# Seven of twenty B products on GpSimd replaced by scalings in token layout, two more C products on GpSimd

## The chip, the cores and the metric

One core of a Trainium2 chip. The metric is the device time of one execution, in microseconds. The kernel before was run three times without the profiler: 3344.13, 3342.19 and 3343.15 us, median 3343.15. The names of the engines in rows: PE is TensorE (PEld its weight loads), DVE is VectorE, ACT is ScalarE, POOL is GpSimd, SP is the engine that issues most DMAs.

## The reference, cut to what matters

```
xn = layernorm(x)                                  # x: 32 batch rows, 512 tokens, 256 channels
for each of two directions (forward, backward in time), with its own weights:
    delta, B, C = split(xn @ x_proj_w.T)           # 32, 16 and 16 columns
    delta = softplus(delta @ dt_proj_w.T + dt_proj_b)      # token x 256
    for each of 16 states n:
        h_t = exp(delta_t * A_n) * h_(t-1) + delta_t * B_t,n * xn_t
        y_t += h_t * C_t,n
    y += D * xn
g = silu(xn + 0.3 * (one expert's MLP of xn, the expert chosen by the last token))
out = x + (y_forward + y_backward) * g
```

## The kernel before

The 32 batch rows are worked one after the other. A row has 32 steps, one for each pair of direction and state (step s is state s mod 16 of direction s div 16). Channels lie on the partitions, in two halves of 128, and the 512 tokens along the free dimension, so that the tensors of a step are 128 x 1024. Each step needs:

- the decay exp(delta * A_n), two activations on ACT (L745, `make_decay`);
- the data delta * xn * B. In 20 of the steps (POOL_B) it is one product on POOL, dx times a broadcast row of B that SP loads from DRAM to all partitions (`times_b`, L473). In the 12 steps of TURNED it comes another way: dx was turned once per direction to token layout (tokens on partitions, `dxT`), ACT scales it by B as a scalar per partition in four activations of 128 x 256 (`scale_dx`, L584), and PE turns the result back with eight transposes into PSUM (`turn_bx`, L1054). In these steps the decay goes to SBUF (`decay_sb`, two slots) and the data to PSUM; in the others the other way round;
- the scan on DVE over time, `hs` (L849), four slots by step;
- the product with C, `hc`. In 13 steps (POOL_C) POOL makes it from a loaded broadcast row of C (L461), four steps after its own step counter (C_LAG), so POOL's step s does the product of step s - 4. In the other 19 DVE makes it (L827), with C broadcast into one PSUM bank by a matmul (`broadcast_c`, L1062), one step after the scan;
- the addition over states in PSUM, eight transposing matmuls on PE (`add_state`, L1079), for POOL's products two steps late (ADD_LAG).

The order of each engine's work is written out by hand: each engine has a `body` that runs over the 32 steps, and waits on semaphores tie them together. Beside the steps each engine does, at fixed step numbers, its part of the front of the next row (layer norm, projections, step size delta, dx, the expert's MLP, the gate): the constants at the top, such as LOG1P = (25, 36) or DX = (28, 43), are the steps, and a number above 31 is a step of the row itself, 32 less. In POOL's part `log1p` is L448, the step size L453, dx L444, the small products of the layer norm L487 to L493, and the residual L480.

Rings tie the engines together around the change. `bx` has RING = 4 slots: `times_b` number i waits for the scan that read number i - 4. `hs` has 4 slots: scan s waits for the product with C of step s - 4, whichever engine makes it. The two PSUM slots `decay0` and `decay1` are used by step parity: what is written for step s waits for scan s - 2. `turn_bx` of step s is issued at PE's step s - 3, ahead of the additions and of PE's front work.

SP issues the loads of B and C rows some products ahead (BRING = 6, CRING = 5), waiting each time for the product that frees the slot, and between them the row's other transfers, all in one queue.

Ahead of the first step lies a prologue of some 84 us: weights, the router, and products of the experts' second layers (`w2`, `wo`), with the front of row 0 in between.

## Time and profile before

| | |
|---|---|
| median of three runs | 3343.15 us |
| the profiled execution | 3348.41 us |
| its span in the trace | 3346.6 us |
| POOL: bx product (L473) | 640, mean 2380 ns |
| POOL: hc product (L461) | 416, mean 2369 ns |
| ACT: scaling of dx (L584) | 1536, mean 497 ns |
| PE: turns (L1054) | 3072 transposes, 435.5 us |
| mean granted clock of TensorE | 0.92 |

The page of the profile gives for each engine the time in which it was busy. The groups by line give count, mean duration and, behind a second bar, the time in which the engine sat idle just before them, with what ended it. Starts in the trace are in microseconds from the beginning of the span; where two instructions of one engine follow each other at once, the distance of their starts is what one takes of the engine, a little less than its duration.

### The profile page before, as it was taken

To read this page: it belongs to the slowest core of one execution; us is meant where nothing else is said; L and a number is where in the kernel's file an instruction comes from. 1 tells how busy PE (TensorE), PEld (TensorE's weight loads), DVE (VectorE), ACT (ScalarE), POOL (GpSimd) and SP (SyncE) were. 2 spreads that over 40 slices of the span, in tenths; PEclk is the share of its full clock that TensorE was granted. 3 is DMA by queue.
4 is the path that set the end of the run, shared out by engine and by line. 5 is a ranking of instruction groups with operands and counts; after the bars stand their busy time and mean duration, and the time that the engine had idled before them with its cause. 6 is when DMAs were issued, how large, how long until landed. Compare 5 with 4: busy or idle time off the path is not lost. (4 is left out here: it accounts for less than half of the span.)

```text
span 3346.6 us, 47865 instructions
## 1 busy us (share of the span) xinstructions
PE 2561.6 (77%) x15542; PEld 2049.9 (61%) x15542; DVE 3116.1 (93%) x2059; ACT 2908.7 (87%) x5370; POOL 3010.0 (90%) x1422
## 2 busy tenths in 40 slices
PE   7777777777777777777777777777777777777776
PEld 5666656666566665566666566666566665666665
DVE  2899999999999999999999999999999999999998
ACT  4888889989888888898888899898898888898985
POOL 2899999999998998999999999999999889999997
PEclk9898999899899988999889999988999889999888
DMA  5443344442344433434433444423434334344332
GB/s 155 137 125 104 100 138 121 128 124 88 119 131 125 125 109 95 132 121 128 125 103 101 136 122 125 126 91 115 130 128 125 106 93 136 119 130 124 96 104 69
DMA packets 273358, 394.09 MB, mean 118 GB/s; under 512 B 45003, under 2 KB 119508, under 8 KB 273108
## 3 DMA queue, kind: packets, MB, share of 16 engines
q1 hardware_dynamic: 273108, 391.03, 38.1%
q8 instruction: 124, 2.03, 0.2%
q14 instruction: 126, 1.03, 0.1%
HBM read 348.98 MB, written 25.18 MB: 112 GB/s over the span
## 5 line engine op out<-in xcount | busy, mean ns | idle before, releaser
L473 POOL TENSOR_TENSOR bx<-dx,b_sb 128x1024 f32<-128x1024 f32 x640 | 1511.8, 2380 | 99.5 <-DVE hs L849 97.7
L849 DVE TENSOR_TENSOR_SCAN hs<-decay,bx 128x1024 f32<-128x1024 f32 x640 | 1458.0, 2280 | 25.5 <-ACT decay L745 8.5
L1079 PE MATMUL y<-ident,hc 128*128 128x128 f32 x8192 | 1145.4, 291 | 25.7 <-DVE hc L827 25.5
L1079 PEld LDWEIGHTS y<-ident,hc 128*128 128x128 f32 x8192 | 1029.9, 152 | 141.2 <-DVE hc L827 80.1
L461 POOL TENSOR_TENSOR hc<-hs,c_sb 128x1024 f32<-128x1024 f32 x416 | 981.0, 2369 | 13.2 <-DVE hs L849 12.9
L849 DVE TENSOR_TENSOR_SCAN hs<-decay_sb,decay 128x1024 f32<-128x1024 f32 x384 | 865.1, 2274 | 77.1 <-issue 38.0
L745 ACT ACTIVATE decay<-delta,rate 128x512 f32<-128x512 f32 (+1 forms) x1280 | 827.3, 683 | 62.1 <-DVE hs L849 61.7
L827 DVE TENSOR_TENSOR hc<-hs,c 128x1024 f32<-128x1024 f32 x608 | 728.7, 1199 | 40.7 <-PE c L1062 36.8
L584 ACT ACTIVATE dxb<-dxT,btok 128x256 f32<-128x256 f32 x1536 | 651.2, 497 | 0.5 <-PE decay L1054 0.5
L1054 PE MATMUL decay<-ident,dxb 128*128 128x128 f32 x3072 | 435.5, 288 | 252.8 <-DVE hs L849 246.4
L1054 PEld LDWEIGHTS decay<-ident,dxb 128*128 128x128 f32 x3072 | 359.7, 147 | 367.5 <-issue 272.7
L1062 PE MATMUL c<-dbc,selector 128*128 128x512 f32 x608 | 327.0, 538 | 324.8 <-DVE hc L827 324.7
L745 ACT ACTIVATE decay_sb<-delta,rate 128x512 f32<-128x512 f32 (+1 forms) x768 | 506.2, 715 | 0.0
L1062 PEld LDWEIGHTS c<-dbc,selector 128*128 128x128 f32 x608 | 125.1, 206 | 407.8 <-DVE hc L827 389.7
L1023 PE MATMUL front<-w2o_sb,hT 128*128 128x256 f32 x1024 | 287.0, 430 | 77.9 <-issue 77.9
L1023 PEld LDWEIGHTS front<-w2o_sb,hT 128*128 128x128 f32 x1024 | 214.7, 221 | 114.2 <-issue 84.4
L1007 PE MATMUL front<-xnT,w_sb 128*128 128x512 f32 x512 | 249.9, 611 | 44.0 <-ACT delta L596 42.8
L448 POOL TENSOR_TENSOR lg<-lg,ex 128x1024 f32<-128x1024 f32 x64 | 151.1, 2362 | 86.9 <-ACT lg L613 86.9
L592 ACT ACTIVATE ex<-front,dtb 128x512 f32<-128x512 f32 x128 | 87.3, 682 | 100.0 <-PE front L998 99.6
L574 ACT ACTIVATE dxT<-front 128x512 f32<-128x512 f32 x128 | 75.8, 592 | 103.3 <-PE front L983 103.1
L619 ACT ACTIVATE hT<-front,b_sb 128x512 f32<-128x512 f32 x128 | 87.7, 685 | 87.3 <-PE front L1007 87.3
L1007 PEld LDWEIGHTS front<-xnT,w_sb 128*128 128x128 f32 x512 | 88.3, 192 | 121.6 <-issue 63.1
(127 smaller groups left out, 2294.4 us busy)
## 6 DMA issues: line engine op xcount, KB each, us to landing
b_sb<-b_scratch SPq DMA_DIRECT2D x640, 256.0 KB, 3.4
c_sb<-b_scratch SPq DMA_DIRECT2D x416, 256.0 KB, 3.6
xin<-in_L_attn_x_dram SPq DMA_DIRECT2D x32, 512.0 KB, 7.7
w_sb<-in_L_ffn_W_dram SPq DMA_DIRECT2D x32, 512.0 KB, 4.3
w2o_sb<-w2o_scratch SPq DMA_DIRECT2D x32, 512.0 KB
xres<-in_L_attn_x_dram SPq DMA_DIRECT2D x32, 512.0 KB, 5.4
out_dram<-og SPq DMA_DIRECT2D x32, 512.0 KB, 4.4
dbc<-high SPq DMA_DIRECT2D x64, 128.0 KB, 5.6
```

The source lines that it names most:

```text
L448: nc.gpsimd.tensor_tensor(lg[:, :, :], lg[:, :, :], ex[:, g, :, :], ALU.mult).then_inc(s_log1p, 1)
L461: nc.gpsimd.tensor_tensor(hc[:, s % RING, :, :], hs[:, s % HSLOTS, :, :], c_sb[:, i % CRING, :].unsqueeze(1).broadcast_to([P, DT, T]), ALU ...
L473: nc.gpsimd.tensor_tensor(bx[:, i % RING, :, :], dx[:, g, :, :], b_sb[:, i % BRING, :].unsqueeze(1).broadcast_to([P, DT, T]), ALU.mult).th ...
L584: A(dxb[:, (row * NT + i) % XSLOTS, c, :], dxT[:, g, c, :], ACT.Copy, scale=btok[:, par, c, g, n:n + 1]).then_inc(s_dxb, 1)
L745: A(to[:, k, cols], delta[:, g * (1 + par), k, cols], ACT.Exp, scale=rate[:, g, k, n:n + 1]).then_inc(s_decay, 1)
L827: V.tensor_tensor(hc[:, s % RING, :, :], hs[:, s % HSLOTS, :, :], cps[:, :].unsqueeze(1).broadcast_to([P, DT, T]), ALU.mult).then_inc(s_hc, 1)
L849: V.tensor_tensor_scan(hs[:, s % HSLOTS, :, :].rearrange("p k t -> p (k t)")[:, u], factor.rearrange("p k t -> p (k t)")[:, u], data.rearr ...
L1007: ins = M(fps[:, :], w1_sb[:, k, j * P:(j + 1) * P], xnT[:, par, k, :], start=(k == 0), stop=(k == DT - 1))
L1023: M(to, hT[:, j, c * P:(c + 1) * P], w2o_sb[:, j, :], start=(j == 0), stop=False)
L1054: ins = nc.tensor.transpose(dps[s % DSLOTS][:, k, c * P:(c + 1) * P], dxb[:, (row * NT + i) % XSLOTS, c, k * P:(k + 1) * P], ident[:, :])
L1062: M(cps[:, :], selector[:, N + n:N + n + 1].broadcast_to([P, P]), dbc[:, par, g, :], start=True, stop=True).then_inc(s_cps, 1)
L1079: ins = M(yps[:, c, k * P:(k + 1) * P], hc[:, s % RING, k, c * P:(c + 1) * P], ident[:, :], start=False, stop=(s == ADDED[-1]), is_transpo ...
```

## The change

GpSimd gets a second way to the data of a step. For seven states (POOL_X = 7, 10, 12, 23, 26, 29, 31), which were full products with B on POOL, POOL scales dx in token layout by B, four `tensor_scalar` of 128 x 256 each into a new buffer `dxp` of two slots, and PE turns them back as it does ACT's. TURNED grows from 12 to 19 states, POOL_B shrinks from 20 to 13. Two more products with C (states 22 and 25) move from DVE to POOL, 15 in place of 13. The ring of bx has 3 slots in place of 4, that of B rows 5 in place of 6. SP's queue runs over steps in place of B products, and moves B and C at step 14. In the prologue the loads of dt_proj come ahead of two larger ones, a memset that they wait for comes first, one activation of the router comes earlier, and the first GELU comes after the first two decays.

```diff
-    BRING, CRING, C_AHEAD = 6, 5, 3
-    TSLOTS, XSLOTS = 2, 3
+    BRING, CRING, C_AHEAD = 5, 5, 3
+    BXRING, TSLOTS, XSLOTS, PSLOTS = 3, 2, 3, 2
...
-    TURNED, SCALED_AT, TURN_LEAD = (5, 6, 8, 9, 11, 13, 14, 15, 22, 24, 28, 30), (0, 2, 3, 4, 5, 7, 9, 10, 17, 19, 23, 25), 3
+    SCALED, SCALED_AT, TURN_LEAD = (5, 6, 8, 9, 11, 13, 14, 15, 22, 24, 28, 30), (0, 2, 3, 4, 5, 7, 9, 10, 17, 19, 23, 25), 3
+    POOL_X, POOL_X_AT = (7, 10, 12, 23, 26, 29, 31), (3, 6, 9, 19, 22, 25, 28)
+    TURNED = sorted(SCALED + POOL_X)
     POOL_B = [s for s in range(STEPS) if s not in TURNED]
-    POOL_C, C_LAG, ADD_LAG = (2, 4, 5, 7, 9, 10, 11, 12, 16, 18, 20, 26, 27), 4, 2
+    POOL_C, C_LAG, ADD_LAG = (2, 4, 5, 7, 9, 10, 11, 12, 16, 18, 20, 22, 25, 26, 27), 4, 2
...
+        dxp = sb("dxp", [P, PSLOTS, C, D])
...
-        bx = sb("bx", [P, RING, DT, T])
+        bx = sb("bx", [P, BXRING, DT, T])
...
             sp.dma_start(xin[:, :, :], x_rows[0]).then_inc(s_x, 16)
             for g, w in enumerate((xw_f, xw_b)):
                 sp.dma_start(xw_raw[64 * g:64 * g + 64, :], w).then_inc(s_xw, 16)
-            sp.dma_start(w2_in[0][:, :, :], w2_v[0]).then_inc(s_w2[0], 16)
-            sp.dma_start(wo_sb[:, :, :], wo.rearrange("(k p) n -> p k n", p=P)).then_inc(s_wo, 16)
             sp.wait_ge(s_dtz, 1)
             for g, w in enumerate((dtw_f, dtw_b)):
                 for a in range(2):
                     sp.dma_start(dtw_raw[:, g, :, 64 * a:64 * a + R], w.rearrange("(k p) r -> p k r", p=P)).then_inc(s_xw, 16)
+            sp.dma_start(w2_in[0][:, :, :], w2_v[0]).then_inc(s_w2[0], 16)
+            sp.dma_start(wo_sb[:, :, :], wo.rearrange("(k p) n -> p k n", p=P)).then_inc(s_wo, 16)
...
-                for i in range(NBX):
-                    j = i + BRING - 1
-                    if j < NBX:
-                        load_b(row, par, j)
...
+                for s in range(STEPS):
+                    if s in POOL_B:
+                        j = on_bx(s) + BRING - 1
+                        if j < NBX:
+                            load_b(row, par, j)
+                        elif not last:
+                            load_b(row + 1, 1 - par, j - NBX)
+                    if s - C_LAG in POOL_C:
+                        i = on_pool(s - C_LAG) + C_AHEAD
+                        if i < NPC:
+                            load_c(row, par, i)
+                        elif not last:
+                            load_c(row + 1, 1 - par, i - NPC)
...
-                used = i - RING
+                used = i - BXRING
                 wait(pool, s_scan, used // NBX * STEPS + POOL_B[used % NBX] + 1)
...
+            def scale_dx(row, par, i):
+                g, n, a = POOL_X[i] // N, POOL_X[i] % N, row * NX + i
+                pool.wait_ge(s_btok, row + 1)
+                pool.wait_ge(s_dxT, row * 4 + g * 2 + 2)
+                if a >= PSLOTS:
+                    pool.wait_ge(s_bxT, turned_before(POOL_X, a - PSLOTS))
+                for c in range(C):
+                    nc.gpsimd.tensor_scalar(dxp[:, a % PSLOTS, c, :], dxT[:, g, c, :], btok[:, par, c, g, n:n + 1], None,
+                                            ALU.mult).then_inc(s_dxp, 1)
...
                     if s in POOL_B:
                         times_b(row, s)
                     if s - C_LAG in POOL_C:
                         times_c(row, s - C_LAG)
+                    if s in POOL_X_AT:
+                        scale_dx(row, par, POOL_X_AT.index(s))
                     front(row, par, s + STEPS)
...
-            gelu(0)
-            act.preload_act_table_set(exp_ln)
...
             make_decay(0, 0, 1)
+            gelu(0)
+            act.preload_act_table_set(exp_ln)
```

## Rows read from the trace of the kernel before

**Rows 1.** The page: busy time, share of the span, instructions of each engine.

```profile
PE 2561.6 (77%) x15542; PEld 2049.9 (61%) x15542; DVE 3116.1 (93%) x2059; ACT 2908.7 (87%) x5370; POOL 3010.0 (90%) x1422
```

**Rows 2.** Groups by line and form: count, busy us, mean ns, idle before them.

```profile
L473 POOL TENSOR_TENSOR bx<-dx,b_sb 128x1024 f32<-128x1024 f32 x640 | 1511.8, 2380 | 99.5 <-DVE hs L849 97.7 <-PE y L1079 1.7
L849 DVE TENSOR_TENSOR_SCAN hs<-decay,bx 128x1024 f32<-128x1024 f32 x640 | 1458.0, 2280 | 25.5 <-ACT decay L745 8.5 <-issue 8.3 <-POOL bx L473 6.6
...
L849 DVE TENSOR_TENSOR_SCAN hs<-decay_sb,decay 128x1024 f32<-128x1024 f32 x384 | 865.1, 2274 | 77.1 <-issue 38.0 <-ACT decay_sb L745 31.6 <-POOL hc L461 7.4
...
L745 ACT ACTIVATE decay<-delta,rate 128x512 f32<-128x512 f32 x640 | 437.8, 684 | 27.3 <-DVE hs L849 26.9
...
L745 ACT ACTIVATE decay_sb<-delta,rate 128x512 f32<-128x512 f32 x384 | 274.6, 715 | 0.0
```

**Rows 3.** Timeline of DVE, output products of two rows: start us, us, instruction.

```profile
1621.65 1.20 DVE L820 TENSOR_TENSOR og<-y,gate 128x1024 f32<-128x1024 f32 x1
...
1722.90 1.20 DVE L820 TENSOR_TENSOR og<-y,gate 128x1024 f32<-128x1024 f32 x1
```

**Rows 4.** List of waits: waiting line and releaser, total us, times, longest.

```profile
POOL nwt L487 <- ACT rsq L540: 106.2, 32, 6.3
...
DVE hc L827 <- PE c L1062: 36.8, 33, 1.9
...
PE c L1106 <- DMA decay_sb<-_L_attn_dt_proj_b_w_dram: 10.8, 1, 10.8
```

**Rows 5.** Timeline of DVE, steps 16 to 31 of the same row.

```profile
1665.01 2.28 DVE L849 TENSOR_TENSOR_SCAN hs<-decay,bx 128x1024 f32<-128x1024 f32 x1
1667.21 1.20 DVE L827 TENSOR_TENSOR hc<-hs,c 128x1024 f32<-128x1024 f32 x1
...
1704.12 2.27 DVE L849 TENSOR_TENSOR_SCAN hs<-decay,bx 128x1024 f32<-128x1024 f32 x1
...
1713.51 1.22 DVE L827 TENSOR_TENSOR hc<-hs,c 128x1024 f32<-128x1024 f32 x1 [0.50 <-DVE hs L849]
1715.55 1.22 DVE L827 TENSOR_TENSOR hc<-hs,c 128x1024 f32<-128x1024 f32 x1 [0.82 <-PE c L1062]
```

**Rows 6.** Timeline of POOL, the same row.

```profile
1661.85 9.35 POOL L473 TENSOR_TENSOR bx<-dx,b_sb 128x1024 f32<-128x1024 f32 x4
1671.16 2.35 POOL L461 TENSOR_TENSOR hc<-hs,c_sb 128x1024 f32<-128x1024 f32 x1
```

**Rows 7.** Groups by form: short instructions on POOL.

```profile
L489 POOL TENSOR_SCALAR nwt<-nwt 128x4 f32<-128x4 f32 x32 | 7.1, 221 | 6.3 <-POOL nwt L487 6.3
...
L487 POOL TENSOR_TENSOR nwt<-rsq,nvar 128x4 f32<-128x4 f32 x32 | 6.4, 201 | 106.2 <-ACT rsq L540 106.2
...
L434 POOL MEMSET decay_sb<- 128x512 f32 x1 | 0.5, 518 | 0.0
...
L428 POOL MEMSET eps<- 128x1 f32 x1 | 0.1, 89 | 0.0
```

**Rows 8.** Timeline of ACT, the ratio that log1p waits for.

```profile
1685.13 1.15 ACT L613 ACTIVATE lg<-lg,ratio_shift 128x1024 f32<-128x1024 f32 x1
```

**Rows 9.** Timeline of PE, the same row.

```profile
1652.37 1.06 PE L1054 MATMUL decay<-ident,dxb 128*128 128x128 f32 x8 [0.78 <-DVE hs L849]
...
1704.35 1.06 PE L1054 MATMUL decay<-ident,dxb 128*128 128x128 f32 x8 [2.68 <-DVE hs L849]
1707.55 0.79 PE L1062 MATMUL c<-dbc,selector 128*128 128x512 f32 x1 [2.14 <-DVE hc L827]
1708.14 3.62 PE L1079 MATMUL y<-ident,hc 128*128 128x128 f32 x16
```

**Rows 10.** A window: us, busy PE, PEld, DVE, ACT, POOL; PEclk; DMA share, GB/s.

```profile
1709.00:1711.00 2.00, 2.00 (x11) 2.00 (x11) 2.00 (x3) 0.43 (x1) 2.00 (x2) 0.50 0.03 11
```

**Rows 11.** Timeline of the prologue, up to the first scan.

```profile
78.26 1.28 ACT L623 ACT_TABLE_LOAD   x1
...
84.30 2.29 DVE L849 TENSOR_TENSOR_SCAN hs<-decay,bx 128x1024 f32<-128x1024 f32 x1 [4.93 <-ACT decay L745]
```

More of the change, by code:

```diff
@@ L396, in body @@
                 first, second_last = isinstance(row, int) and row == 0, isinstance(row, int) and row == NB - 2
-                for i in range(NBX):
-                    j = i + BRING - 1
-                    if j < NBX:
-                        load_b(row, par, j)
-                    elif not last:
-                        load_b(row + 1, 1 - par, j - NBX)
-                    for s in POOL_C:
-                        ahead = POOL_C.index(s) + C_AHEAD
-                        if on_bx(s) == i and ahead < NPC:
-                            load_c(row, par, ahead)
-                        elif on_bx(s) == i and not last:
-                            load_c(row + 1, 1 - par, ahead - NPC)
-                    if POOL_B[i] == 10:
+                for s in range(STEPS):
[11 more added lines that the diff above has]
+                            load_c(row + 1, 1 - par, i - NPC)
+                    if s == 10:
                         if not first:
@@ L414, in body @@
                             load_expert(row + 1)
-                    if POOL_B[i] == 16 and not last:
+                    if s == 14 and not last:
                         if not second_last:
@@ L425, in _ @@
         def _(pool):
+            nc.gpsimd.memset(dtw_raw[:, :, :, :], 0.0).then_inc(s_dtz, 1)
             nc.gpsimd.memset(ident[:, :], 0.0).then_inc(s_ident0, 1)
@@ L839, in scan @@
                     dve.wait_ge(s_bx, i + 1)
-                    data, factor = bx[:, i % RING, :, :], dps[s % DSLOTS][:, :, :]
+                    data, factor = bx[:, i % BXRING, :, :], dps[s % DSLOTS][:, :, :]
                 if s in EDGED:
@@ L1049, in turn_bx @@
                 s = TURNED[i]
-                pe.wait_ge(s_dxb, row * C * NT + C * i + C)
+                if s in SCALED:
+                    a = row * NA + SCALED.index(s)
+                    scaled, slot = dxb, a % XSLOTS
+                    pe.wait_ge(s_dxb, C * a + C)
+                else:
+                    a = row * NX + POOL_X.index(s)
+                    scaled, slot = dxp, a % PSLOTS
+                    pe.wait_ge(s_dxp, C * a + C)
                 wait(pe, s_scan, row * STEPS + s - DSLOTS + 1)
```

26 lines of the change are left out of this document (15 added, 11 removed).

## The prediction

> **What bounds the kernel now.** I read the busy table first [rows 1]: DVE 93%, POOL 90%, ACT 87%, PE 77%. No engine leaves room, so the question is which wait ends last at each place. The groups by line [rows 2] give the price of each kind of work. The rows of DVE's output product [rows 3] give the length of one batch row: 1722.90 - 1621.65 = 101.25 us. DVE's idle time in a row divides, by the idle time in its groups [rows 2] and the list of waits [rows 4], into c from PE 36.8/32 = 1.15 us, decay_sb from ACT 31.6/32 = 1.0, and 38.0/32 = 1.2 that is put down to "issue" before the scans of turned states. POOL waits 3.3 us a row for rsq (106.2/32) [rows 4] and 3.1 for scans (97.7/32) [rows 2], and both are signs that it is ahead of DVE there. So DVE sets the time as a whole, and POOL can do so where its own order of work has no slack.
>
> **Price of a step.** Starts give what an instruction really takes of its engine. DVE [rows 5]: scan to product 2.20 (1665.01 to 1667.21), product to scan 1.11. POOL [rows 6]: four products in 1671.16 - 1661.85 = 9.31 us, 2.33 each. PE [rows 9]: the 8 transposes of a turned state take 1.06 us.
>
> **The change, part by part.**
>
> 1. DVE loses the products with C of states 22 and 25: 2 x 1.11 = 2.2 us a row. The scans stay 32, at 2280 or 2274 ns, whether the data is in SBUF or PSUM [rows 2]: nothing.
>
> 2. POOL loses 7 products with B and gains 2 with C: 5 x 2.33 = 11.65 us less a row. It gains 7 x 4 = 28 scalings of 128x256 by a scalar per partition. No row shows one. Nearest rows [rows 7]: a tensor_scalar of 4 elements takes 221 ns (its scalar is a constant), memsets 89 ns at 1 element and 518 at 512, which is 0.84 ns an element. Low end: a memset of 256 elements, 89 + 255 x 0.84 = 303 ns. High end: each element costs what a two-input product's does, (2380 - 201)/1020 = 2.14 ns, so 221 + 252 x 2.14 = 760 ns. With memset's slope on the 4-element tensor_scalar it is 221 + 252 x 0.84 = 433 ns, and I take that: it is the row of the same operation, and one input streams rather than two. Starts on POOL are about 0.045 us closer than durations (2.38 against 2.33), so a scaling costs t = 0.385 us of POOL, between 0.26 and 0.71. A state's four cost 1.54 against 2.33. In sum 28 x 0.385 = 10.8 against 11.65: POOL's total hardly moves.
>
> The Trainium skill's GPSIMD Engine Reference (Performance versus the Vector engine) has one-input bodies at about one cycle an element and two-input ones at 2.6; the two-input slope of the trace, 2.14 ns or 2.6 cycles at the page's 1.2 GHz, agrees, and no run here shows the other yet. By that rule 256 elements would take an estimated 0.22 us of stream beside the dispatch, which leaves the sum where it is.
>
> 3. Where it counts is the order on POOL. With BXRING 3 instead of RING 4 the product bx(19) may start only when scan 16 has ended (the third B product before it is now 16). Scan 16 ends at 1667.2 [rows 5]. State 25's product with C is now POOL's, issued at its step 29, and scan 29 waits for it (it writes the slot of hs that 25 had). From scan 16's end to that release POOL has, in order: bx19, scale 23, bx20, c16, bx21, c18, scale 26, c20, bx25, scale 29, log1p, c22, bx27, step size, scale 31, dx, c25. That is 13 products and 4 states' scalings: 13 x 2.33 + 16 x 0.385 = 30.3 + 6.2 = 36.5 us, with an estimated 0.1 for the hand-over 36.6. No other wait lies inside: log1p needs ACT's ratio, done at 1686.28 [rows 8], and by the sum POOL arrives there at 1688. DVE now needs 1704.12 - 1667.21 = 36.9 us from the end of scan 16 to the start of scan 29 [rows 5] and would need 36.9 - 2.2 = 34.7. So scan 29 starts 0.3 us earlier than now, not 2.2: POOL ends last there, and 1.9 of the 2.2 us is given back. Each 0.01 us of t is worth 0.16 us here, 5.1 us in 32 rows.
>
> 4. The first half: POOL loses bx7, bx10, bx12 and gains three scalings, is ahead by some 2.4 us there and waits for scans; the shorter ring makes bx3 and bx4 wait one scan more, inside the present wait before rsq. Nothing; if that cover goes (rsq 3.3 us), it costs what POOL's lateness exceeds.
>
> 5. PE gains 7 turns, 7 x 1.06 = 7.4 us a row, and loses 2 broadcasts of c: from 77% to some 83%. In the first half they fall where PE waits for scans now (0.78 us before the turn at 1652.37 [rows 9]). A turn waits for the scan two before its own, so it has one scan (2.2 us) in which to finish: 1.1 us to spare. Nothing, between 0 and 0.5 us a row. At the end of the row the turn of 31 (1.1 us) enters a chain in which DVE already waits for c: 0.50 and 0.82 us before the last two products [rows 5]. That chain is slow now because PE runs it at a granted clock of 0.50 [rows 10], the lower of the two levels (1.2 GHz), after 2.68 and 2.14 us of waiting with one turn between: two states' additions, 16 transposes, take 3.62 us where the clock at 1.00 would give 2 x 1.06 = 2.1 [rows 9]. The change puts turn 29 and the addition of state 25 ahead of that gap. If the clock holds, PE saves 1.5 us and pays 1.1 for turn 31; DVE regains 0.5 us of the 1.15 (the transposes of dx in the same stretch give the other 0.1). If it falls all the same, turn 31 costs 1.1 to 1.8 (3.62/2) more. I take the gain of 0.5, between a gain of 1.15 and a loss of 1.8.
>
> The Trainium skill's TensorE: Matmul & The Clock Gate (The HAM clock gate) says that activity releases the throttle; the trace agrees in that the slow stretch follows the idle one.
>
> 6. ACT: seven more decays go to decay_sb, 14 x (0.715 - 0.684) = 0.43 us more [rows 2], and two edge writes fewer (11 to 9). Nothing. Some decays between 8 and 14 may start one scan later than now, since turned states alternate between two slots; ACT makes them two steps ahead, so the cover is one scan. Between 0 and 1.0, as much as decay_sb costs now.
>
> 7. SP: 7 broadcasts of B fewer, 2 of C more, and the move of B and C two steps earlier. All b loads run four products ahead; the queue waits for the low part at its step 14, before any load that POOL needs soon. Nothing; the list of waits has no wait of POOL for a load now, and a late load would show as one.
>
> 8. Prologue: the GELU with its two table loads (from 78.26 on, some 4.5 of the 6.0 us to scan 0; the rest is its decay) moves behind the first two decays; scan 0 waits 4.93 us now [rows 11]. Part of it comes back, since it now stands before decay 2. The dt_proj loads go ahead of two 512 KB loads, and PE waits 10.8 us for them [rows 4]. I take 3 us gained, between 0 and 6.
>
> **Sum.** Per row -0.3 - 0.5 = -0.8 us, x 32 = -26; prologue -3: -29. The profiled execution took 3348.4 us (span 3346.6), 5 above the median of the runs; from it 3319, and from the median 3343.2 - 29 = 3314, the forecast.
>
> **Rivals.**
>
> A, scaling costs more than its stream. A read per partition of the scalar, which the 4-element row with its constant doesn't have, adds a start price as large as that row stands above a memset of 1 element, 221 - 89 = 0.13 us, less the overlap of starts: t = 0.495. Then POOL's chain of step 3 is 1.8 us longer, 38.4, and scan 29 is 1.5 us later than now; with the 0.5 of PE a row is 1.0 longer: +32 - 3 = +29, 3372 us. It decides from t = 0.435, where -0.3 - 0.5 becomes zero. Against it: a tiny two-input product (201 ns) is no dearer than the one-input one (221). At the high end, 0.71, POOL is 5.2 us later in a row, 4.4 net: +138, 3481.
> The Trainium skill's GPSIMD Engine Reference (Performance pitfalls for Q7 kernels) puts about 102 cycles on each small read command that doesn't pipeline, which speaks for this rival; no row here shows it.
>
> B, POOL doesn't bind. With t at 0.26 the chain is 30.3 + 4.2 + 0.1 = 34.6, just DVE's 34.7. A row gains 2.2 + 0.5 = 2.7: -86 - 3, 3254 us. For it: the memset row. Against it: a scaling also reads. Half way, t = 0.32, gives 3283.
>
> C, PE becomes late at the end of the row. The clock falls in the gap before the additions as now, and turn 31 adds between its 1.06 at full clock and 1.8 at the lower level to DVE's wait for c, say 1.4: -0.3 + 1.4 = +1.1, x 32 = +35, - 3: 3375 us. It decides from a wait that grows by 0.4. For it: the gap after turn 30 stays some 2 us; against it: more transposes before.
>
> D, the parts cancel (t about 0.43, or PE's gain absent with a small loss in the first half): 3343 within 6 us.
>
> **Chances.** Forecast 0.38 (its own range 3296 to 3333), B with its half-way cases 0.22, A 0.20, C 0.08, D 0.12. A measurement of this kernel can tell about 0.2%, 7 us. Faster: forecast, B and 0.01 of D, 0.61. Slower: A and C, 0.28 less 0.01 at their near edge, 0.27. Same: the rest, 0.12. The 8 in 10 range leaves out the fastest of B and the slowest of A: 3262 to 3382.
>
> **What would show it.** The scaling's mean in the groups by line: 433 ns carries everything; above 490 ns A, below 370 B. In the list of waits, scans of hs should show a new wait on POOL's hc of some 1.9 us a row, at scan 29. If that is near zero and DVE is faster by 2 us a row, step 3 is wrong (the chain has slack I didn't see). PE's additions near the end of a row at some 2.0 and not 3.6 us show step 5; waits for c above 1.15 us a row refute it. POOL's busy sum near 3000 us confirms step 2. A first scan before 82 us shows step 8. A wait of POOL on b_sb, or of ACT's decays on scans of several us a row, would refute 7 or 6.

## The result

The changed kernel takes 3688.55 us (median of 4 runs, 3678.91 to 3691.67) against 3343.64 for the kernel before in the same comparison: a ratio of 1.1022, 95% interval 1.1003 to 1.1042. Forecast were 3314 us, range 3262 to 3382. The profiled execution has a span of 3677.1 us and a mean granted TensorE clock of 0.897 (0.916 before). Of three kernels in part 7 single executions ran 40 to 70 us faster than the others of the same kernel, and their medians are not used for a difference.

The page's busy line of the changed kernel, to be held against [rows 1]:

```profile
PE 2799.4 (76%) x17270; PEld 2280.1 (62%) x17270; DVE 3062.4 (83%) x1995; ACT 2916.3 (79%) x5306; POOL 3439.0 (94%) x2158
```

DVE's work fell by 54 us (93 to 83% of a longer span), and POOL's rose by 429 us where step 2 expected it to stay near 3000. The groups by line (count, busy us, mean ns, idle before them), beside [rows 2]:

```profile
L873 DVE TENSOR_TENSOR_SCAN hs<-decay_sb,decay 128x1024 f32<-128x1024 f32 x608 | 1374.9, 2278 | 351.0 <-POOL hc L470 216.4 <-ACT decay_sb L767 93.8 <-issue 26.3
...
L482 POOL TENSOR_TENSOR bx<-dx,b_sb 128x1024 f32<-128x1024 f32 x416 | 984.9, 2386 | 170.9 <-DVE hs L873 165.9 <-DMA b_sb<-b_scratch 4.9
L873 DVE TENSOR_TENSOR_SCAN hs<-decay,bx 128x1024 f32<-128x1024 f32 x416 | 945.9, 2280 | 105.5 <-POOL hc L470 98.2 <-ACT decay_sb L767 3.8 <-ACT decay L767 3.2
L493 POOL TENSOR_SCALAR dxp<-dxT,btok 128x256 f32<-128x256 f32 x896 | 814.1, 935 | 0.0
L851 DVE TENSOR_TENSOR hc<-hs,c 128x1024 f32<-128x1024 f32 x544 | 651.8, 1198 | 69.3 <-PE c L1093 69.3
```

The line to look at is L493, the new scaling: 935 ns, where I had put 433 and an upper bound of 760. The products kept their price. DVE's scans, which hardly waited for POOL before, now wait 216.4 + 98.2 = 314.6 us for its products with C. The list of waits (total us, times, longest) says the same from the other side, and of POOL's wait for rsq, 106.2 us in [rows 4], only 5.9 are left:

```profile
DVE hs L873 <- POOL hc L470: 314.6, 131, 5.7
DVE hs L873 <- ACT decay_sb L767: 97.6, 72, 3.8
DVE hc L851 <- PE c L1093: 69.3, 59, 1.4
...
POOL nwt L506 <- ACT rsq L561: 5.9, 1, 5.9
```

POOL's timeline in one row (start us, us, instruction). The three bx at 1821.78 end with bx19, the three hc at 1868.74 begin with c25:

```profile
1821.78 7.06 POOL L482 TENSOR_TENSOR bx<-dx,b_sb 128x1024 f32<-128x1024 f32 x3
1828.80 3.64 POOL L493 TENSOR_SCALAR dxp<-dxT,btok 128x256 f32<-128x256 f32 x4
1832.38 2.39 POOL L482 TENSOR_TENSOR bx<-dx,b_sb 128x1024 f32<-128x1024 f32 x1
...
1868.74 6.98 POOL L470 TENSOR_TENSOR hc<-hs,c_sb 128x1024 f32<-128x1024 f32 x3
1875.68 7.04 POOL L482 TENSOR_TENSOR bx<-dx,b_sb 128x1024 f32<-128x1024 f32 x3
1886.73 2.37 POOL L482 TENSOR_TENSOR bx<-dx,b_sb 128x1024 f32<-128x1024 f32 x1 [4.01 <-DVE hs L873]
```

DVE's scans 16 and 29 in that row, and the output products of all rows, before and after:

```profile
1822.85 2.28 DVE L873 TENSOR_TENSOR_SCAN hs<-decay,bx 128x1024 f32<-128x1024 f32 x1
...
1871.22 2.29 DVE L873 TENSOR_TENSOR_SCAN hs<-decay_sb,decay 128x1024 f32<-128x1024 f32 x1 [3.99 <-POOL hc L470]
```

```profile
L820 DVE TENSOR_TENSOR og<-y,gate x32: 1198/1198/1226, 198.2 to 3339.5; 128x1024 f32<-128x1024 f32 x32
L844 DVE TENSOR_TENSOR og<-y,gate x32: 1196/1198/1223, 207.3 to 3670.0; 128x1024 f32<-128x1024 f32 x32
```

Four scalings take (1832.38 - 1828.80) = 3.58 us of POOL, t = 0.895 each from start to start. Added up, POOL's work in a row is 35 products x 2.33 + 28 x 0.895 + 1.15 for the small instructions = 107.8 us, and one wait, 4.01 at 1886.73, before the product bx3, makes it 111.8. The 32 output products of DVE start from 207.3 to 3670.0 us, 111.70 a row. Work and waits of an engine always add up to the row; what tells is that one wait is all that POOL has left, so its own work, plus that one wait, is the row. The 31 row lengths account for 31 x (111.70 - 101.33) = 321 us of the 330.5 by which the span grew (before, from 198.2 to 3339.5, a row was 101.33), and the later first product (207.3 against 198.2) for the other 9.

### The profile page after: what moved, and what is told of

It is laid out like the page before. It is cut to its first block and busy times, and to the rows that moved or that the text cites. A ratio compares the mean times of both kernels' runs of the same rounds, so it can differ in the third digit from the quotient of the medians.

```text
span 3677.1 us, 51895 instructions
## 1 busy us (share of the span) xinstructions
PE 2799.4 (76%) x17270; PEld 2280.1 (62%) x17270; DVE 3062.4 (83%) x1995; ACT 2916.3 (79%) x5306; POOL 3439.0 (94%) x2158
## 5 line engine op out<-in xcount | busy, mean ns | idle before, releaser
L873 DVE TENSOR_TENSOR_SCAN hs<-decay_sb,decay 128x1024 f32<-128x1024 f32 x608 | 1374.9, 2278 | 351.0 <-POOL hc L470 216.4
L482 POOL TENSOR_TENSOR bx<-dx,b_sb 128x1024 f32<-128x1024 f32 x416 | 984.9, 2386 | 170.9 <-DVE hs L873 165.9
L470 POOL TENSOR_TENSOR hc<-hs,c_sb 128x1024 f32<-128x1024 f32 x480 | 1129.6, 2371 | 0.9 <-PE y L1110 0.8
L873 DVE TENSOR_TENSOR_SCAN hs<-decay,bx 128x1024 f32<-128x1024 f32 x416 | 945.9, 2280 | 105.5 <-POOL hc L470 98.2
L767 ACT ACTIVATE decay_sb<-delta,rate 128x512 f32<-128x512 f32 (+1 forms) x1216 | 803.3, 713 | 151.1 <-DVE hs L873 151.0
L493 POOL TENSOR_SCALAR dxp<-dxT,btok 128x256 f32<-128x256 f32 x896 | 814.1, 935 | 0.0
L851 DVE TENSOR_TENSOR hc<-hs,c 128x1024 f32<-128x1024 f32 x544 | 651.8, 1198 | 69.3 <-PE c L1093 69.3
L767 ACT ACTIVATE decay<-delta,rate 128x511 f32<-128x511 f32 (+1 forms) x832 | 539.4, 684 | 41.6 <-DVE hs L873 41.2
L1085 PE MATMUL decay<-ident,dxb 128*128 128x128 f32 x3072 | 421.6, 282 | 111.7 <-DVE hs L873 109.9
L1085 PE MATMUL decay<-ident,dxp 128*128 128x128 f32 x1792 | 264.4, 296 | 16.9 <-DVE hs L873 16.9
L1085 PEld LDWEIGHTS decay<-ident,dxp 128*128 128x128 f32 x1792 | 225.7, 153 | 67.4 <-issue 49.3
```

Of the source, the lines that this page charges most:

```text
L470: nc.gpsimd.tensor_tensor(hc[:, s % RING, :, :], hs[:, s % HSLOTS, :, :], c_sb[:, i % CRING, :].unsqueeze(1).broadcast_to([P, DT, T]), ALU ...
L482: nc.gpsimd.tensor_tensor(bx[:, i % BXRING, :, :], dx[:, g, :, :], b_sb[:, i % BRING, :].unsqueeze(1).broadcast_to([P, DT, T]), ALU.mult). ...
L493: nc.gpsimd.tensor_scalar(dxp[:, a % PSLOTS, c, :], dxT[:, g, c, :], btok[:, par, c, g, n:n + 1], None, ALU.mult).then_inc(s_dxp, 1)
L767: A(to[:, k, cols], delta[:, g * (1 + par), k, cols], ACT.Exp, scale=rate[:, g, k, n:n + 1]).then_inc(s_decay, 1)
L851: V.tensor_tensor(hc[:, s % RING, :, :], hs[:, s % HSLOTS, :, :], cps[:, :].unsqueeze(1).broadcast_to([P, DT, T]), ALU.mult).then_inc(s_hc, 1)
L873: V.tensor_tensor_scan(hs[:, s % HSLOTS, :, :].rearrange("p k t -> p (k t)")[:, u], factor.rearrange("p k t -> p (k t)")[:, u], data.rearr ...
```

## The experiments

Three questions: is the scaling itself the cause and what makes it dear (parts 1, 2 and 5), do the prediction's other steps hold once it is cheap (2 to 4), and what is then left (6 and 7)? Kernels that have a line fewer or more are shifted by it (L872 is L873). Code cuts leave out the indentation and what stands around them.

**1. The operation alone, and with a constant.** One kernel runs nothing but GpSimd, each form four times. The other is the changed kernel with this edit, which leaves B out for the seven states:

```
-  nc.gpsimd.tensor_scalar(dxp[...], dxT[:, g, c, :], btok[:, par, c, g, n:n + 1], None, ALU.mult)
+  nc.gpsimd.tensor_scalar(dxp[...], dxT[:, g, c, :], 0.5, None, ALU.mult)
```

> A kernel of its own that computes nothing of the reference: GpSimd alone runs each form four times back to back while the other engines rest. The forms are tensor_scalar times a scalar per partition on 4, 128, 256 and 1024 elements, times a constant on 4, 256 and 1024, tensor_copy on 256 and 1024, tensor_tensor on 256 and 1024, and tensor_tensor with the scalar spread as second input, on 256 and on 4 x 256 in one instruction. Theory 1, every element of a tensor_scalar is slow: 256 elements take about 935 ns as in the changed kernel, 1024 about 3.1 us, 128 about 580 ns, with the constant the same. Theory 2, reading the scalar per partition has a start price of 0.5 us: 4 elements with it take about 720 ns, 256 with a constant 430 ns, 1024 with it 1.6 us. Theory 3, the other engines' traffic makes it slow in the kernel: alone 256 elements take about 430 ns in either form.

> The changed kernel, where GpSimd's scaling multiplies by the constant 0.5 in place of B's column (what is left out: B for seven states). Theory 1 (slow elements): the scaling stays near 935 ns and the time near 3690 us. Theory 2 (the scalar's read): 430 ns, GpSimd does 28 x 0.5 = 14 us less in a row, and the time falls to 3330 to 3350 us. Theory 3 (contention): 935 ns as in theory 1.

Groups by form of the first (col is a factor read from a column, one per partition; L59 and L60 have a constant; L66 is a two-input product whose second operand is four such columns, each spread over 256 elements):

```profile
L57 POOL TENSOR_SCALAR o<-a,col 128x1024 f32<-128x1024 f32 x4 | 11.3, 2842 | 0.1
L60 POOL TENSOR_SCALAR o<-a 128x1024 f32<-128x1024 f32 x4 | 11.0, 2768 | 0.1
L64 POOL TENSOR_TENSOR o<-a,b 128x1024 f32<-128x1024 f32 x4 | 9.2, 2338 | 0.1
L66 POOL TENSOR_TENSOR o<-a,col 128x1024 f32<-128x1024 f32 x4 | 7.5, 1899 | 0.1
L62 POOL COPY o<-a 128x1024 f32<-128x1024 f32 x4 | 4.0, 1040 | 0.1
L56 POOL TENSOR_SCALAR o<-a,col 128x256 f32<-128x256 f32 x4 | 3.6, 922 | 0.1
L59 POOL TENSOR_SCALAR o<-a 128x256 f32<-128x256 f32 x4 | 3.3, 852 | 0.1
L63 POOL TENSOR_TENSOR o<-a,b 128x256 f32<-128x256 f32 x4 | 2.8, 722 | 0.1
...
L61 POOL COPY o<-a 128x256 f32<-128x256 f32 x4 | 1.4, 399 | 0.1
```

With nothing beside it the scaling takes 922 ns, against 935 in the kernel: it is the instruction, not contention. The column costs 922 - 852 = 70 ns. What costs is the stream: (2842 - 922)/768 = 2.50 ns an element, where a copy has (1040 - 399)/768 = 0.83 and a full product (2338 - 722)/768 = 2.10. With the constant the changed kernel had scalings of 863 ns and took 3587.0 us, ratio 1.0731 (1.07 to 1.0761): most of the loss stays, so the column isn't the main cause. (The 102 us that went are more than the 896 x 0.072 = 65 us of work; the rest was not followed.)

The Trainium skill's GPSIMD Engine Reference (Performance versus the Vector engine) has one-input bodies at about one cycle an element, which is 0.83 ns at the page's 1.2 GHz. For the copy the trace agrees (0.83 ns); for this scaling, one input too, it doesn't (2.50 ns), and the measurement decides.

**2. Other ways to make or to skip the scaling.** First one two-input product per state in place of four scalings; then a copy in its place, which leaves B out for seven states; then no turned states on GpSimd at all, but 15 products with C.

```
+  nc.gpsimd.tensor_tensor(dxp[...], dxT[:, g, :, :],
+                          btok[:, par, :, g, n:n + 1].broadcast_to([P, C, D]), ALU.mult)
```

> The changed kernel, where one tensor_tensor of 128 x 1024 with B's four columns spread over 256 elements each takes the place of the four tensor_scalar. If a two-input product costs the 2.33 us that it does elsewhere, whatever its second input's strides, a state costs 2.33 and not 3.59 us, a row 7 x 1.26 = 8.8 us less as long as GpSimd sets the time: 3689 - 280 = 3409 us. If the spread input is slow, the time stays or grows. The view that GpSimd's total is not what binds (PE's turns are) expects no more than 50 us of gain.

```
+  nc.gpsimd.tensor_copy(dxp[:, a % PSLOTS, c, :], dxT[:, g, c, :])
```

> The changed kernel, where GpSimd's four scalings of a state are four copies of the same 128 x 256 (what is left out: B for seven states). Alone a copy took 399 ns, starts 0.355 us apart, so this is the change as the prediction priced it (433 ns, 0.385 us), with all else in place. If only the price of the scaling was wrong, the prediction's own sum holds: 16 x 0.03 = 0.5 us a row better than its -0.8, so -1.3 x 32 - 3 = -45: 3299 us, between 3270 and 3333. If its other steps were wrong too (turns on PE, decays of turned states, the ring of 3), the time is 3343 us or more, and the list of waits says which.

```
-  BRING, CRING, C_AHEAD = 5, 5, 3
-  BXRING, TSLOTS, XSLOTS, PSLOTS = 3, 2, 3, 2
+  BRING, CRING, C_AHEAD = 6, 5, 3
+  BXRING, TSLOTS, XSLOTS, PSLOTS = 4, 2, 3, 2
...
-  POOL_X, POOL_X_AT = (7, 10, 12, 23, 26, 29, 31), (3, 6, 9, 19, 22, 25, 28)
+  POOL_X, POOL_X_AT = (), ()
```

> The changed kernel without GpSimd's scalings: the seven states are full products with B again (bx ring of 4, B rows ring of 6), the rest of the change stays, with 15 products with C on GpSimd. If the scalings are the loss, it is gone: GpSimd has 42 products of 2.33 us in a row, 98 us with the small ones, against 101.25 us of row before. In the order of work, scan 29 then waits for the product with C of state 25 some 0.9 us longer than it starts now, so a row is about 1 us longer than before the change: 3375 us, between 3343 and 3410. If PE's or ACT's part of the change were the loss, it would be gone too (both return to twelve turned states), so this run tells the scalings and turns from the products with C, the queue and the prologue: those expect 3600 or more if they are the cause.

| kernel | a state's scaling on POOL | us | ratio (95%) |
|---|---|---|---|
| spread product | 1913 ns | 3371.7 | 1.0085 (1.0063 to 1.0107) |
| copy | 4 x 409 ns | 3319.7 | 0.993 (0.9915 to 0.9945) |
| 15 C, full products | none | 3366.0 | 1.0072 (1.005 to 1.0094) |

The spread product takes 37 us less than the 3409 expected of it, which went by 2.33 us a state. The copy run tests everything in the prediction but the price. Its group, its waits, and POOL and DVE around scans 16 and 29 of a row:

```profile
L493 POOL COPY dxp<-dxT 128x256 f32<-128x256 f32 x896 | 322.0, 409 | 0.1
```

```profile
DVE hs L872 <- PE decay L1084: 64.9, 80, 1.6
...
DVE hc L850 <- PE c L1092: 21.1, 18, 1.4
DVE hs L872 <- POOL hc L470: 15.3, 10, 1.5
```

```profile
1689.23 7.07 POOL L470 TENSOR_TENSOR hc<-hs,c_sb 128x1024 f32<-128x1024 f32 x3
```

```profile
1655.54 1.20 DVE L850 TENSOR_TENSOR hc<-hs,c 128x1024 f32<-128x1024 f32 x1
...
1691.79 2.29 DVE L872 TENSOR_TENSOR_SCAN hs<-decay_sb,decay 128x1024 f32<-128x1024 f32 x1 [1.25 <-PE decay L1084]
```

With a price near the one I had assumed (409 against 433 ns) the kernel takes 3320 us, six above the forecast and inside the forecast's own range (but 20 above what its expectation gave for the copy's price). Scan 16 ended at 1655.54, where DVE's next product starts, and c25 at 1689.23 + 2.33 = 1691.56: 36.0 us, where step 3's formula with this copy's 1.39/4 = 0.3475 gives 13 x 2.33 + 16 x 0.3475 + 0.1 = 35.95. What ends last before scan 29 is then a turn of PE, for which DVE waits 1.25 us, a wait the prediction didn't have. It is a close thing: scan 29 starts at 1691.79, 0.23 us after c25. The last row of the table is worse than before, too: 15 products with C beside 20 with B leave POOL 120.2 us late for DVE's scans.

**3. The ring of bx, with the dear scaling.**

```
-  BRING, CRING, C_AHEAD = 5, 5, 3
-  BXRING, TSLOTS, XSLOTS, PSLOTS = 3, 2, 3, 2
+  BRING, CRING, C_AHEAD = 4, 4, 3
+  BXRING, TSLOTS, XSLOTS, PSLOTS = 4, 2, 3, 2
```

> The changed kernel with four slots of bx again, for which the rings of B and C rows go to 4 each. GpSimd waits 4.0 us a row before the B product of state 3, which now needs scan 0; with four slots it needs scan 27. If GpSimd's work with that wait makes up the row (107.8 + 4.0 = 111.8 us), the wait goes and nothing takes its place: up to 4.0 x 32 = 128 us less, 3561 to 3600 us. If the row is bound by scans and turns instead, the wait only moves, and the time stays at 3680 or more. Loads that come late for the smaller rings would show as waits of GpSimd for DMA.

3586.3 us, ratio 1.0724 (1.0709 to 1.0739), 102 us less than the change. POOL no longer waits for scans before bx, and the output products came 108.7 us apart, where POOL's work is 107.8: with the dear scaling POOL's sum of work is the row, and the ring adds most of the rest. Of the 4.0 us a row that went, part comes back as a wait for rsq (45.1 us in all, 5.9 with three slots).

**4. The parts of the change that have nothing to do with the scaling.** One kernel with the change's order of SP's queue and its prologue, but 13 products with C and full products with B as before; one with the prologue alone.

```
-  for i in range(NBX):
-      j = i + BRING - 1
...
+  for s in range(STEPS):
+      if s in POOL_B:
+          j = on_bx(s) + BRING - 1
...
+      if s - C_LAG in POOL_C:
+          i = on_pool(s - C_LAG) + C_AHEAD
...
-  if POOL_B[i] == 16 and not last:
+  if s == 14 and not last:
```

> The kernel before with the change's prologue and SP queue alone: no scalings on GpSimd, 13 products with C, rings of before. The changed kernel's first scan starts 3.4 us earlier than before but its fourth only 0.3 us earlier, so the prologue is worth between 0 and 3 us: 3340 to 3344 us. If the queue in steps makes loads or the moves late, it is 3350 or more.

> The kernel before with the change's prologue alone; SP's queue is that of before. Prologue and queue together gave 3324 us. The first output product starts 3.3 us earlier there than before, and rows are 0.6 us shorter. If the queue makes the rows shorter, this run is only 3 us quicker than before: 3340 us. If something of the prologue carries into the rows (a phase of the engines against each other), it is 3324.

3324.2 us, ratio 0.994 (0.9926 to 0.9954), and 3344.1, 0.9995 (0.9984 to 1.0006). The first missed its expectation of 3340 to 3344. So the prologue brings nothing, and SP's new order together with the earlier move of B and C (the two were not told apart) some 20 us, which step 7 had put at nothing. The groups of DVE's scans in the first of them:

```profile
L872 DVE TENSOR_TENSOR_SCAN hs<-decay,bx 128x1024 f32<-128x1024 f32 x640 | 1456.3, 2280 | 10.3 <-ACT decay L766 5.9 <-issue 0.2
L872 DVE TENSOR_TENSOR_SCAN hs<-decay_sb,decay 128x1024 f32<-128x1024 f32 x384 | 865.2, 2274 | 77.6 <-issue 38.3 <-POOL hc L469 24.9 <-ACT decay_sb L766 14.4
```

Against [rows 2] the idle time before scans of bx is 25.5 - 10.3 = 15.2 us less: the waits put down to POOL's bx (6.6 us) and to "issue" (8.3) are gone, and those for decay_sb are halved (31.6 to 14.4). Part of that comes back as waits for POOL's products with C (7.4 to 24.9). PE's wait for the transfer of the low part of B and C (`dbc<-low`) also fell, from 8.2 us with the prologue alone to 1.4. Why the new order helps was not followed further.

**5. Why it is dear.** The forms once more, with a second operation in one of them:

```
L54  tensor_scalar(dst(1024), flat, 0.5, None, ALU.add)
L55  tensor_scalar(dst(1024), flat, 0.5, 1.0, ALU.mult, ALU.add)
L62  tensor_tensor(dst(1024), flat, flat, ALU.mult)
```

> A kernel of its own that computes nothing of the reference: GpSimd alone, each form four times. Alone a tensor_scalar of 1024 elements took 2842 ns, a tensor_tensor of two full inputs 2338, one with a repeated scalar as second input 1899, a copy 1040. Here: tensor_scalar with add, with two operations, with the scalar per partition on 1024 and 512; tensor_tensor with one scalar spread over 1024, with a 512 row used twice (the B product's form), with the same tensor twice, and 4 columns spread over 256 each. If the cost is a second operation slot that tensor_scalar always runs, one and two operations take the same 2.8 us. If it is the multiply, add is quicker. If the spread form is quick because its second input is read from few addresses, the same tensor twice stays at 2.3 us and the 512 row at 2.3.

```profile
L56 POOL TENSOR_SCALAR o<-a,col 128x1024 f32<-128x1024 f32 x4 | 11.3, 2845 | 0.1
L54 POOL TENSOR_SCALAR o<-a 128x1024 f32<-128x1024 f32 x4 | 11.0, 2772 | 4.8 <-DMA b<-in_L_attn_x_dram 4.8
...
L62 POOL TENSOR_TENSOR o<-a 128x1024 f32<-128x1024 f32 x4 | 7.4, 1893 | 0.1
...
L55 POOL TENSOR_SCALAR o<-a 128x1024 f32<-128x1024 f32 x4 | 4.1, 1047 | 0.1
```

A tensor_scalar that does two operations takes 1047 ns, one that does a single operation 2772: the one with more to do is 2.65 times as quick, and as quick as a copy. So the dear thing is the form with a single operation; why it is dear is not shown. The product of a tensor with itself (L62) takes 1893 ns, as little as the spread one, so the few addresses of the spread column aren't what makes that quick. In the changed kernel the second operation is one edit:

```
-  btok[:, par, c, g, n:n + 1], None, ALU.mult)
+  btok[:, par, c, g, n:n + 1], 1.0, ALU.mult, ALU.mult)
```

> The changed kernel with each of its 28 scalings a row written with two operations (times B, then times 1.0) in place of one; the product is the same. Theory 1 (the one-operation form is what is dear): the scaling falls from 935 ns to 380 to 450 ns, as the copy of the same tile (409 ns) and the two-operation form of 1024 elements (1047 ns, a copy of 1024 being 1040) say; the time is that of the copy experiment, 3320 us (3300 to 3340), a row 100.5 us. Theory 2 (multiplying by a factor read from a column is dear in any form, and the quick one was so for its constants): the scaling stays above 850 ns and the time at 3640 to 3700 us.

3375.6 us, ratio 1.0092 (1.0067 to 1.0118): 313 us less than the change, with the same design. Its group, DVE's main wait, and its chain on POOL and DVE:

```profile
L493 POOL TENSOR_SCALAR dxp<-dxT,btok 128x256 f32<-128x256 f32 x896 | 415.8, 489 | 0.0
```

```profile
DVE hs L873 <- POOL hc L470: 114.5, 63, 3.4
DVE hc L851 <- PE c L1093: 42.9, 50, 1.2
```

```profile
1680.28 2.40 POOL L482 TENSOR_TENSOR bx<-dx,b_sb 128x1024 f32<-128x1024 f32 x1 [2.98 <-DVE hs L873]
1682.63 1.86 POOL L493 TENSOR_SCALAR dxp<-dxT,btok 128x256 f32<-128x256 f32 x4
1684.45 2.39 POOL L482 TENSOR_TENSOR bx<-dx,b_sb 128x1024 f32<-128x1024 f32 x1
...
1715.56 6.98 POOL L470 TENSOR_TENSOR hc<-hs,c_sb 128x1024 f32<-128x1024 f32 x3
```

```profile
1718.04 2.29 DVE L873 TENSOR_TENSOR_SCAN hs<-decay_sb,decay 128x1024 f32<-128x1024 f32 x1 [2.97 <-POOL hc L470]
```

Theory 1's account of the price holds in the main, but the scaling is 489 ns and not the copy's 409 (the column's 70 ns would be most of that), and the time lies above the 3300 to 3340 it gave. This is the place and the wait of step 3: bx19 starts when scan 16 has ended, c25 is done at 1715.56 + 2.33 = 1717.89, 37.6 us later (the formula with (1684.45 - 1682.63)/4 = 0.455 gives 30.3 + 7.3 = 37.6), and scan 29 starts with it, 2.97 late. From the copy to this form t grows by 0.1075, which by step 3 is 16 x 0.1075 x 32 = 55 us; measured are 56 (3319.7 to 3375.6). That it fits so closely is in part luck: the output products are 100.44 and 102.00 us apart in the two traces, 1.56 x 31 = 48 us, and c25 had 0.23 us to spare in the copy run.

**6. Taking the chain away.** The two-operation kernel with the ring edit of part 3:

> The kernel of m13_two_operations with four buffers for products with B in place of three (the rings of B's and C's broadcasts go from 5 to 4 for the room). Theory 1 (the chain from scan 16 through 13 products and 16 scalings is what is left): VectorE's waits for GpSimd's products with C (114.5 us in m13) fall under 30 us, and the time falls to that of the copy experiment or below, 3290 to 3330 us. Theory 2 (GpSimd has too much work in that stretch whatever starts it, or its waits only move): those waits stay above 80 us and the time within 15 us of m13's 3376.

3288.2 us, ratio 0.9831 (0.981 to 0.9852): 87 us less than with the ring of three. Its waits of DVE:

```profile
DVE hs L873 <- PE decay L1085: 66.6, 90, 1.6
...
DVE hs L873 <- POOL hc L470: 13.4, 29, 0.5
DVE hc L851 <- PE c L1093: 9.6, 8, 1.2
```

Waits for POOL fell from 114.5 to 13.4 us, as theory 1 had it. Waits for PE's turns rose from 21.3 to 66.6 and are now the largest, and those for c fell from 42.9 to 9.6 while the granted clock went from 0.942 to 0.966, so not all of the 87 us need be the chain's.

**7. TensorE's clock.** Three kernels have 14 products with C on GpSimd: the kernel of part 4 with c22 added, and the changed kernel with c25 back on DVE, once with the spread product and once with two operations.

> Prologue and queue of the change, no scalings on GpSimd, and one more product with C on GpSimd, that of state 22: 14. From the trace of before, with the step from the ratio on: c22, bx26, bx27, step size, dx, bx29, c26, bx31, c27, all of 2.33 us after log1p ends at 1688.7; bx29 is then done at 1702.7 where scan 29 starts at 1703.0 without VectorE's product 22, and c27 at 1709.7 where scan 31 starts at 1709.6. So nothing of the 1.11 us is given back but 0.1: 3324 - 32 x 1.0 = 3292 us, between 3280 and 3324. If GpSimd's total is what binds, as 15 products did (3366), it is 3324 or more.

> The spread product in place of the scalings (3372 us), and state 25's product with C back on VectorE, so 14 on GpSimd. In the trace of the spread product scan 29 waits 3.5 us in each row for that product. If it is this wait that holds the row, it goes, GpSimd has 2.33 us less ahead of the next product, and VectorE 1.1 us more: some 2.4 us less in a row, 77 us, 3295 us, between 3280 and 3335. If the wait is only an image of GpSimd's total (which falls by 2.33 too) the gain is alike, but if VectorE, ACT or PE bind, the 1.1 us more makes it 3372 + 35 = 3407 us.

> The kernel of m13_two_operations with the product with C of state 25 back on VectorE (14 on GpSimd). Theory 1: scan 29 no longer waits for c25, GpSimd is freed of 2.33 us a row, VectorE gains 2.2 us of work and sheds its wait; with TensorE's clock as in the spread product with 14 (0.953) the time is 3300 to 3335 us. Rival (VectorE's work is the row now, so that 2.2 us of product cost what they take): 40 to 70 us above m13. Under theory 2 of m13 it is 3560 to 3640 us.

The first missed its expectation of 3292: 3367.2 us, ratio 1.0062 (1.0045 to 1.0078), 43 above the kernel with 13, at a granted clock of 0.898 (0.918 with 13). The second took 3329.6 to 3330.4 us in three runs at a clock of 0.953 and 3263.7 in one at 0.99; the third 3328.9 to 3336.5 in three at 0.952 or 0.953 and 3273.7 in one at 0.974. The same instructions, some 60 us apart, and the clock apart with them; both traces are of slower executions, so what differs was not seen. What they show is that without c25 on POOL the scans' waits for its products are gone: 11.3 us in the second, 118.8 with c25 on POOL, and 11.0 in the third, against 114.5. To see whether the clock is the handle, PE gets work whose result nobody reads, at step 27, behind the row's last ReLU:

```
+  if s == 27 and not last:
+      pe.wait_ge(s_relu, (row + 1) * 4 + 4)
+      for _ in range(16):
+          nc.tensor.transpose(fps[:, 0:P], ident[:, :], ident[:, :])
```

> As m11, and PE turns the identity 16 times into the free front bank at the end of its step 27, where it waits some 2 us for VectorE before the slow additions. If those additions are slow because the granted clock falls after that wait, it now stays at 1.00 there, VectorE's wait for c before its last two products (1.2 us a row) goes, and the time is 20 to 40 us below m11's. If the clock falls for what lies earlier, or the extra work comes in the way, the time is that of m11 or 10 to 30 us more.

> The kernel of m13_two_operations with 16 transposes of the identity on TensorE at step 27 of each row, behind the row's last ReLU, whose results nobody reads. If TensorE's clock (0.96 in the copy experiment) is what makes decay 22 and 29 late, the granted clock rises to 0.97 to 1.0 and the time falls by 15 to 50 us against m13 (3270 to 3305 us). If GpSimd's order sets the row instead, nothing is won: within 8 us of m13; and the 16 transposes delay TensorE's own work by at most 1.5 us a row if they are in its way (45 us more).

> Both edits, c25 on VectorE and the 16 transposes. If the run of the spread product at clock 0.99 (3264 us) shows what TensorE's clock leaves, the time is 3250 to 3290 us at a clock of 0.98 or more, under both kernels. If VectorE's own work sets the row whatever the clock, it is 3300 us or more.

> The kernel of m17 with the 16 transposes of the identity at step 27 of each row. With the chain gone TensorE's turns are the last to end: a clock of 0.97 or more brings 15 to 50 us against m17 (3250 to 3305 us). If GpSimd's order still sets the row it is within 8 us of m17, as m15 (3370) was of m13 (3376).

| kernel | without, us (clock) | with the 16 transposes, us (clock) |
|---|---|---|
| 14 C, full products | 3367.2 (0.898) | 3316.6 (0.944), ratio 0.9914 (0.9896 to 0.9931) |
| two operations | 3375.6 (0.942) | 3370.0 (0.951), ratio 1.0078 (1.0053 to 1.0103) |
| two operations, c25 on DVE | 3328.9 to 3336.5 (0.952, 0.953) in three, 3273.7 (0.974) in one | 3314.6 to 3317.9 (0.971) in three, 3272.7 (0.98) in one |
| two operations, ring of 4 | 3288.2 (0.966) | 3283.0 (0.973), ratio 0.9816 (0.9795 to 0.9836) |

PE's timeline of the first without the transposes, and with them:

```profile
1718.55 3.62 PE L1109 MATMUL y<-ident,hc 128*128 128x128 f32 x16
```

```profile
1790.07 3.27 PE L1233 MATMUL front<-ident 128*128 128x128 f32 x16
...
1793.42 1.91 PE L1109 MATMUL y<-ident,hc 128*128 128x128 f32 x16
```

and two windows of the stretch with them, with the columns of [rows 10]:

```profile
1790.00:1793.00 3.00, 3.00 (x17) 3.00 (x16) 3.00 (x3) 3.00 (x5) 3.00 (x2) 0.53 0.40 147
1793.00:1797.00 4.00, 4.00 (x37) 3.86 (x35) 3.86 (x3) 2.37 (x6) 4.00 (x3) 1.00 0.21 70
```

The added transposes themselves run at the lower level (3.27 us for 16, granted clock 0.53), behind them it is 1.00, and the additions behind them take 1.91 us for 16, which took 3.62 without. In the kernel with 14 C and full products that is worth 51 us, more than the 20 to 40 that was expected. Of the 52 us between the two spans DVE's groups show 46: 24.5 less idle before its products with C (waits for c 41.8 before, 1.0 now), 13.9 less before turned scans, and 7.4 in two others. In the kernel with c25 on DVE both columns have two levels, the faster one alike (3273.7 and 3272.7), so the row shows no gain that can be told from them. Where POOL's chain sets the row, or with the ring of 4, the 6 and 5 us lie within the intervals: the gains of 15 to 50 us that these two were expected to have if the clock counted did not come. The lowest medians of all, 3283 and 3288 us, are those of the change with two operations and four bx buffers, 1.7 to 1.8% under the kernel before and 11% under the changed one; single executions with c25 on DVE were faster (3263.7, 3273.7, 3272.7), at clocks of 0.974 to 0.99.

## Why the prediction was wrong

**Step 2, the step that failed.** Its mechanism stood (fewer products, 28 scalings in their place); the price of a scaling was mis-sized. I took 433 ns, from memset's 0.84 ns an element on the 4-element tensor_scalar of [rows 7], and 760 as the high end, taking it for granted that an element of one input can't cost more than one of two. Measured: 935 ns, 2.50 ns an element, above the two-input product. Memset's slope was right for a copy (0.83) and nearly for the form with two operations, where the whole scaling is 489 ns. The row I leaned on was the same operation, but at 4 elements it holds no slope, so its range was no bound at all. POOL's 28 scalings are 25.1 us a row, not 10.8, and where they were to balance the 11.65 removed, 13.4 are lost: 13.4 x 32 = 429 us, by which POOL's busy time did grow.

**Step 3, the chain, was right near the planned price, and not enough.** In the run with two operations bx19 waits 2.98 us for scan 16, and c25 releases scan 29. In the copy run PE's turn ends last, 0.23 us behind c25. In the changed kernel c25 still releases scan 29, but bx19 doesn't wait: it starts at 1826.44 (the third bx from 1821.78), when scan 16 has been done since 1825.05 (1822.85 + 2.20). From there to c25's end at 1868.74 + 2.33 = 1871.07 it is 44.6 us, as the formula says (13 x 2.33 + 16 x 0.895 = 44.6), but what comes before bx19 is POOL's own work too. So the formula, which counts 16 scalings of the 28, falls short. Carried on to t = 0.895 it gives 3314 + 16 x 0.51 x 32 = 3575 us; measured were 3689. POOL has no idle time left but the wait before bx3, and its whole sum counts, 28 x t and not 16. From t = 0.455 to 0.895 the row grew by 9.7 us (102.0 to 111.7): 28 x 0.44 = 12.3, less the (239.5 - 165.9)/32 = 2.3 of POOL's waits for scans that this used up, makes 10.0.

**Step 4** put the first half at nothing, the ring of 3 included, because POOL's wait for rsq would cover it. The cover is gone in every trace with the ring of 3 (5.9 us in all, once, in the changed kernel, the two-operation and the copy run): POOL waits for a scan before bx3 instead. (The 3.1 us a row that the prediction read as POOL's waits for scans before the change hold one single wait of 24.8; without it they are 2.3.) In the copy run that does no harm that shows (DVE's waits for POOL are 15.3 us in all). In the changed kernel it comes on top of POOL's full sum, and four slots take 102 us off (part 3).

**Step 5.** Two parts. PE's turns were to cost 0 to 0.5 us a row: in the copy run the waits of scans for PE's decay are 64.9/32 = 2.0, in the two-operation run with four bx buffers 2.1. The end of the row was to gain 0.5: in the change 16 additions there take 3.02 us (2.0 forecast, 3.62 before), at a granted clock of 0.50 and then 0.69, the waits for c rose from 1.15 to 69.3/32 = 2.2 us a row, and the mean clock fell to 0.897. That PE idles more when POOL is late, and so loses its clock, is argued and was not tested by itself. In the copy run the additions take 2.19 and the waits fell to 21.1/32 = 0.7, the gain as forecast. The Trainium skill's TensorE: Matmul & The Clock Gate (The HAM clock gate) says that activity releases the throttle. The run with 14 C and the added transposes agrees: 0.53 while they ran, 1.00 behind them.

**Step 6** (ACT: 0 to 1.0, taken as nothing): decay_sb is late by 30.7/32 = 0.96 in the copy run, 31.6/32 before; right. In the change it is 97.6/32 = 3.0. ACT itself waits 151.0 us there for the scans that free decay_sb (58.5 in the copy run), so late scans fit as the reason, but that was not tested.

**Step 7** (SP: nothing) missed a gain of 20 us. The waits that went were in [rows 2], as POOL's bx and "issue".

**Step 8** (prologue: -3): scan 0 starts at 80.85 and not 84.30, but scan 2 then waits 2.41 us for the decay that stands behind the GELU, scan 3 starts at 95.06 against 95.35 before, and the run of the prologue alone is at 0.9995. Nothing.

**Rivals and chances.** A had the sign and the place. Its time, 3372 for a price of 0.495, is met by the two-operation run (3376) and the spread product (3372), but at prices of 0.455 and 0.465, for which the prediction's own sum gives 3350 and 3355: that fit is luck. Its reason, the read of a column, is 70 ns of the 500 that were missing. Its upper end, 3481, lay 208 us too low, and the range's, 3382, by 307. No run had the price of B (0.26), and C's longer waits for c are not in the copy run. For the copy's 0.3475 the prediction's own sum is 3314 - 16 x 0.0375 x 32 = 3295 us, and the run is 25 above. The errors named above (PE's turns +2.0 a row, SP's order -0.6, the prologue +3) would make 48 of it: their signs fit, their sum overshoots, and the waits of one kind may stand in part in place of others. It stays open how much each is worth, and that the copy run came within six of the forecast is luck as well. The prediction said that L493's mean "carries everything", and it did.

## What to carry to other kernels

Before a plan rests on many small instructions of a form that the trace doesn't hold, time that form alone at its real size: a few elements show the start and nothing of the slope. A bound taken from "less to do can't take longer" is a guess as well; here the same operation was 2.6 times quicker at 1024 elements, and 1.9 times in the kernel, once it was given a second one to do. And a chain that is worked out for the planned price is only a lower bound beyond it: check at which price the engine's whole sum takes over.

## What was unexpected of the hardware

- GpSimd, fp32, 128x1024: tensor_scalar with one operation 2768 to 2845 ns, with two operations and constants 1047, a copy 1040, a product of two tensors 2338 or 2340. At 128x256 with the factor in a column: one operation 922 to 935, two 489.
- A two-input product is cheaper when its second operand is a spread column (1893 to 1913 ns) or the first tensor again (1893) than with two different ones (2338).
- Sixteen transposes that nobody reads, put where TensorE was idle, made a kernel 51 us quicker (granted clock 0.898 to 0.944), and one kernel with c25 on VectorE ran at 3330 us in three executions and at 3264 in one, at clocks of 0.953 and 0.99. What decides between those two was not found.
